# First attention: where the output projection waits for the four pieces of its weight

## The chip, the cores and the metric

One core of one Trainium2 chip runs the whole program in one launch. The metric is the device time in microseconds. The kernel before took 1580.31 us, the median of three runs (1579.23 to 1580.67).

## The reference

The reference computes four residual layers on x of shape (2, 512, 512): attention with 32 heads in 8 key/value groups, a gated feed-forward layer with ternary weights, a second attention with 32 small heads, and a routed low-rank layer. Only the first attention matters here. Cut to its core it is:

```python
q = (h @ wq.T)   # 32 heads of 128; h is the layer norm of x
k = (h @ wk.T)   # 8 heads of 128, each shared by 4 query heads
v = (h @ wv.T)
q, k = rotary(q), rotary(k)
scores = einsum(q, k) / sqrt(128) * scale + causal
attn = einsum(softmax(scores), v)          # (2, 512, 4096)
x = x + attn @ wo.T                        # wo: (512, 4096)
```

## The kernel before, in words

Every matrix product is done in three TensorE matmuls on values split into a high and a low part (`product`, line 59 on: lines 64, 65 and 66 are hi times hi, lo times hi, hi times lo). So every weight that arrives from HBM is split by GpSimd in two instructions, line 403 for the high part and line 405 for the low part, before TensorE may use it; the second one counts `piece_split` up by one.

The first attention (`attention0_phase`) runs over 8 groups g, one for each key/value head. A group has 8 steps s, one for each unit of attention (2 batches times 4 query heads). Group 0 is written out, groups 1 to 6 are a loop, group 7 is written out, and 4 more steps follow it, in which only output projections are left. Each engine has its own program, and all orders are written out by hand; the engines meet in semaphores.

In a step TensorE does two score tiles of the next unit, two transposes (line 562, seven matmuls), then the side work of the step, then two more score tiles, half of a query projection, two parts of the attention output, a transpose and so on. The side work (`SIDE`) is keys in steps 0 and 4, values in steps 1 and 5, and the output projection (`make_out`) in steps 2, 3, 6 and 7. Steps 6 and 7 project batch 0 of this group, steps 2 and 3 batch 1 of the group before it. One step has two halves, that is two token tiles; each half sums four products, one for each head j, and each product is three matmuls of 512 columns. So `make_out` issues 12 matmuls for a half. After each half VectorE adds the bank to x (line 736).

The group's piece of the output weight comes in four pieces, one for each head j: `PIECES` gives ("wo", 0) and ("wo", 1) to step 4 and ("wo", 2) and ("wo", 3) to step 5. SP fetches each into one of five raw slots, and GpSimd splits it in that step: it does the low part of the query of the step before (line 421), then the pieces, then the sum of the next rotation (line 411). `free_for` lets it overwrite the output weight once the last output projection of the group before is done (step 3).

`make_out` has its waits in the first half of steps 2 and 6 alone: for the attended heads (`attended_split`, counted by VectorE), and for `piece_split` at the count of the fourth piece, both ahead of the first product. Step 2 uses the same weight as step 6 before it. There are 8 executions of step 6 with an output projection and 8 of step 2.

Of the kernel before, what the change touches and what calls it, by code (L numbers as in the profile page):

```python
# [29 lines left out]
PER_KV = HEADS0 // KV0  # L30
# [24 lines left out]
def wait(engine, semaphore, value):  # L55

    if isinstance(value, int) and value <= 0:
        return
    engine.wait_ge(semaphore, value)


def product(nc, out, left, right, start, stop):

    nc.tensor.matmul(out, left[0], right[0], start=start, stop=False)  # L64
    nc.tensor.matmul(out, left[0], right[1], start=False, stop=False)  # L65
    return nc.tensor.matmul(out, left[1], right[0], start=False, stop=stop)  # L66
# [146 lines left out]
def attention0_phase(nc, m):  # L213
    dram = m.dram
    with ExitStack() as ctx:
# [3 lines left out]
        def pair(what, shape):  # L219
            return sb(f"{what}_hi", shape, F32R), sb(f"{what}_lo", shape, F32R)  # L220

        def sem(what):
            return ctx.enter_context(nc.semaphore(f"a0_{what}"))
# [6 lines left out]
        wo = pair("wo", [P, PER_KV, D])  # L230
# [24 lines left out]
        piece_hi, piece_split = sem("piece_hi"), sem("piece_split")  # L255
# [30 lines left out]
        def piece_count(g, what, which):  # L286

            names = [x[:2] for x in PIECES]
            return len(FIRST_PIECES) + len(PIECES) * g + names.index((what, which)) + 1
# [33 lines left out]
        def wait_output_bank(pe, g, s, what, half):  # L323

            at = OUTPUTS.index((s, what, half)) - 2
            gb = g
            while True:
                if at < 0:
                    at, gb = at + len(OUTPUTS), gb - 1
                sb_, before, hb = OUTPUTS[at]  # L330
                if isinstance(gb, int) and gb < 0:
                    return
                if present(gb, sb_, before):
                    break
                at -= 2
            if before == "out":
                wait(pe, out_added, out_count(gb, sb_, hb))
            else:
                wait(pe, attended_split, GROUP * gb + sb_ + 1)
# [137 lines left out]
        def _(pe):  # L477
# [20 lines left out]
            def weights_ready(what, which, g):  # L498

                if isinstance(g, int) and g == 0 and what != "wo":  # L500
                    return FIRST_PIECES.index((what, which)) + 1
                if what == "wo":
                    if isinstance(g, int) and g == KV0 - 1:
                        return len(FIRST_PIECES) + len(PIECES) * g + which + 1
                    return piece_count(g, what, which)
                return piece_count(g - 1, what, which)
# [72 lines left out]
            def make_out(g, s, half):  # L579

                b = 1 if s < 4 else 0
                t = 2 * (s % 2) + half
                bank = OUTPUTS.index((s, "out", half)) % 2
                gw = g - 1 if b else g
                wait_output_bank(pe, g, s, "out", half)
                if half == 0 and s in (2, 6):
                    wait(pe, attended_split, GROUP * gw + PER_KV * (b + 1))
                    wait(pe, piece_split, weights_ready("wo", PER_KV - 1, gw))
                for j in range(PER_KV):
                    at = slice(t * P, (t + 1) * P)  # L590
                    last = product(nc, ps_out[:, bank, :], (attended[0][:, b, j, at], attended[1][:, b, j, at]),
                                   (wo[0][:, j, :], wo[1][:, j, :]), j == 0, j == PER_KV - 1)
                last.then_inc(out_made, 1)

            def step(g, s):
# [7 lines left out]
                if present(g, s, SIDE[s]):  # L603
                    if SIDE[s] == "out":
                        make_out(g, s, 0)
                        make_out(g, s, 1)
                    elif SIDE[s] == "keys":
                        make_keys(g, s)
                    else:
                        make_values(g, s)  # L610
# [1484 lines left out]
```

## Time and profile before

| | |
|---|---|
| median of 3 runs | 1580.31 us |
| the profiled execution's own time | 1577.87 us |
| its span, first to last instruction | 1576.0 us |
| TensorE matmul busy | 1457.7 us, 92% of the span |
| VectorE, ScalarE, GpSimd busy | 1020.9, 857.8, 536.7 us |
| mean granted TensorE clock | 0.977 of full speed |

Times in the rows count from the start of the span. In a row of the timeline "[1.79 <-POOL a_wo_lo L405]" means that the engine had been idle for 1.79 us before the instruction, and that line 405 on GpSimd released it. PE is TensorE's matmuls and PEld its weight loads; the load of a matmul's weights runs beside the matmul before it.

### The profile page before, as it was taken

The numbers are of one execution on the slowest core, as the hardware profiler recorded it, in microseconds if no ns is written. First come the engines' busy times: TensorE is split into PE (matmuls) and PEld (weight loads), VectorE is DVE, ScalarE is ACT, GpSimd is POOL, SyncE is SP. The second block draws the span as 40 slices with busy tenths as digits, with TensorE's granted clock in tenths as the row PEclk, the third lists the DMA queues.
The fourth block names the chain that finished last, engine by engine and source line by source line (L and its number), as shares of the span: only waits on it lengthen the run. The fifth ranks groups of instructions, "written<-read, shape, count | busy, mean of one in ns | idle before, by whom it ended". The sixth has DMA issues, their size and how long they took to land. (4 is left out here: it accounts for less than half of the span.)

```text
span 1576.0 us, 25393 instructions
## 1 busy us (share of the span) xinstructions
PE 1457.7 (92%) x7696; PEld 1205.1 (76%) x7696; DVE 1020.9 (65%) x2547; ACT 857.8 (54%) x2183; POOL 536.7 (34%) x467
## 2 busy tenths in 40 slices
PE   6899999999999999999887999998789899986798
PEld 4788888888888888888766888886677777764586
DVE  7767667676676766667645333354788888897643
ACT  2766555665556655566523323311888888894210
POOL 5563555545555455553310000023332214010600
PEclk9999999999999999999988999999999999997999
DMA  4010010101101000000002111106433434322000
GB/s 163 14 48 15 27 35 20 40 13 27 33 20 40 13 29 31 27 7 7 15 7 88 61 60 60 54 0 107 94 74 87 73 81 85 73 34 96 21 21 27
DMA packets 37517, 71.98 MB, mean 46 GB/s; under 512 B 4992, under 2 KB 5376, under 8 KB 36864
## 3 DMA queue, kind: packets, MB, share of 16 engines
q1 hardware_dynamic: 29664, 55.35, 11.4%
q0 software_dynamic: 7776, 15.73, 6.3%
q8 instruction: 33, 0.54, 0.1%
q14 instruction: 44, 0.36, 0.1%
HBM read 60.58 MB, written 10.49 MB: 45 GB/s over the span
## 5 line engine op out<-in xcount | busy, mean ns | idle before, releaser
L804 ACT ACTIVATE a_probs<-a_probs,a_least 128x512 f32<-128x512 f32 (+3 forms) x256 | 143.0, 559 | 179.6 <-DVE a_least L684 170.9
L411 POOL TENSOR_TENSOR a_rotated<-a_by_cos,a_by_sin 128x512 f32<-128x512 f32 x80 | 103.5, 1293 | 244.3 <-DVE a_by_sin L707 242.2
L692 DVE TENSOR_TENSOR a_probsT_lo<-a_ps_turn,a_probsT_hi 128x512 fp32r<-128x512 f32 (+3 forms) x256 | 118.7, 484 | 72.1 <-ACT a_probsT_hi L812 70.6
L812 ACT CAST a_probsT_hi<-a_ps_turn 128x512 fp32r<-128x512 f32 (+3 forms) x256 | 101.4, 426 | 100.9 <-PE a_ps_turn L562 100.8
L1702 ACT ACTIVATE a_probs<-a_probs,a_least 128x128 f32<-128x128 f32 (+3 forms) x256 | 142.2, 560 | 2.4 <-issue 1.5
L1590 DVE CUSTOM_DVE_ANT_0 a_probs<-f_ps_gate,a_causal 128x128 f32<-128x128 f32 (+3 forms) x256 | 116.9, 486 | 31.2 <-PE f_ps_gate L1447 21.2
L864 ACT ACTIVATE a_probs<-a_probs,a_inverse 128x128 f32<-128x128 f32 (+3 forms) x256 | 123.2, 553 | 8.6 <-DVE a_inverse L717 7.5
L64 PE MATMUL a_ps_out<-a_wo_hi,a_attended_hi 128*128 128x512 f32 x256 | 105.4, 412 | 17.6 <-POOL a_wo_lo L405 15.4
L684 DVE CUSTOM_DVE_ANT_0 a_probs<-a_ps_score,a_causal 128x512 f32<-128x512 f32 (+2 forms) x192 | 101.0, 551 | 29.4 <-PE a_ps_score L66 29.3
L421 POOL TENSOR_TENSOR a_query_lo<-a_rotated,a_query_hi 128x512 fp32r<-128x512 f32 x64 | 82.6, 1290 | 107.9 <-ACT a_query_hi L824 107.9
L736 DVE TENSOR_TENSOR x<-a_ps_out,x 128x512 f32<-128x512 f32 x64 | 44.3, 691 | 104.3 <-PE a_ps_out L66 104.3
L64 PE MATMUL a_ps_proj<-xT_hi,a_wq_hi 128*128 128x512 f32 x256 | 109.1, 426 | 1.5 <-DVE a_values_lo L712 1.5
L1598 DVE TENSOR_TENSOR a_probsT_lo<-f_ps_out,a_probsT_hi 128x384 fp32r<-128x384 f32 (+1 forms) x192 | 108.9, 596 | 2.4 <-ACT a_probsT_hi L1711 2.2
L1460 PE MATMUL f_ps_out<-ident,a_probs 128*128 128x128 f32 x640 | 93.7, 278 | 14.0 <-ACT a_probs L1702 13.8
L562 PE MATMUL a_ps_turn<-ident,a_probs 128*128 128x128 f32 x640 | 102.3, 275 | 2.5 <-ACT a_probs L864 2.5
L65 PE MATMUL a_ps_out<-a_wo_lo,a_attended_hi 128*128 128x512 f32 x256 | 102.5, 400 | 0.0
L66 PE MATMUL a_ps_out<-a_wo_hi,a_attended_lo 128*128 128x512 f32 x256 | 102.4, 400 | 0.0
L1711 ACT CAST a_probsT_hi<-f_ps_out 128x384 fp32r<-128x384 f32 (+1 forms) x192 | 85.8, 511 | 30.4 <-PE f_ps_out L1460 30.3
L66 PE MATMUL a_ps_proj<-xT_hi,a_wq_lo 128*128 128x512 f32 x256 | 100.7, 393 | 0.0
L65 PE MATMUL a_ps_proj<-xT_lo,a_wq_hi 128*128 128x512 f32 x256 | 100.3, 392 | 0.0
L1460 PEld LDWEIGHTS f_ps_out<-ident,a_probs 128*128 128x128 f32 x640 | 74.3, 142 | 25.7 <-ACT a_probs L1702 11.4
L1447 PE MATMUL f_ps_gate<-a_stacked_k,a_stacked_q 128*128 128x128 f32 (+3 forms) x256 | 76.3, 377 | 16.5 <-DMA a_stacked_k<-in_slope 7.8
(276 smaller groups left out, 4129.2 us busy)
## 6 DMA issues: line engine op xcount, KB each, us to landing
a_raw<-in_wq SPq DMA_DIRECT2D x36, 256.0 KB, 2.7
a_raw<-in_wo SPq DMA_DIRECT2D x36, 256.0 KB, 2.6
a_stacked_q<-a_spill_q POOLq DMA_DIRECT2D x48, 128.0 KB, 5.1
a_stacked_k<-a_spill_k POOLq DMA_DIRECT2D x24, 256.0 KB, 5.1
f_raw<-in_gate SPq DMA_DIRECT2D x14, 256.0 KB, 2.7
f_raw<-in_up SPq DMA_DIRECT2D x14, 256.0 KB, 2.9
f_raw<-in_down SPq DMA_DIRECT2D x14, 256.0 KB, 3.6
a_raw<-in_wk SPq DMA_DIRECT2D x12, 256.0 KB, 2.9
```

The costliest lines, as they stand in the source:

```text
L64: nc.tensor.matmul(out, left[0], right[0], start=start, stop=False)
L65: nc.tensor.matmul(out, left[0], right[1], start=False, stop=False)
L66: return nc.tensor.matmul(out, left[1], right[0], start=False, stop=stop)
L411: nc.gpsimd.tensor_tensor(rotated[:], by_cos[:], by_sin[:], ALU.add).then_inc(rotation_added, 1)
L562: last = nc.tensor.transpose(ps_turn[:, t % 2, (i - t) * P:(i - t + 1) * P], probs[:, u % 2, at:at + P], m.ident[:])
L692: nc.vector.tensor_tensor(probsT[1][:, t % 2, 0:w], ps_turn[:, t % 2, 0:w], probsT[0][:, t % 2, 0:w].bitcast(F32), ALU.subtract).then_inc( ...
L804: nc.scalar.activation(tile, tile, ACT.Exp, bias=least[:, slot, i:i + 1], scale=-1.0, accum_out=total[:, slot, i:i + 1]).then_inc(exp_done, 1)
L864: nc.scalar.activation(tile, tile, ACT.Copy, scale=inverse[:, slot, i:i + 1]).then_inc(probs_ready, 1)
L1460: last = nc.tensor.transpose(ps_turn[:, t, to:to + P], probs[:, u % 4, at:at + P], m.ident[:])
L1590: nc.vector.tensor_tensor_reduce(out=probs[:, u % 4, at:at + w], in0=ps_score[:, i % 2, 0:w], in1=causal[:, SEQ - w:SEQ], scale=-float(HD1 ...
L1598: nc.vector.tensor_tensor(probsT[1][:, u % 2, at], ps_turn[:, t, 0:TURNED_WIDTH[t]], probsT[0][:, u % 2, at].bitcast(F32), ALU.subtract).t ...
L1702: nc.scalar.activation(tile, tile, ACT.Exp, bias=least[:, u % 4, i:i + 1], scale=-1.0, accum_out=total[:, u // 4 % 2, i, u % 4:u % 4 + 1]) ...
```

## The change

The wait for the fourth piece ahead of the first product is taken out. In its place each of the four products has a wait of its own, ahead of its three matmuls, for the count of its own piece. As before this is in the first half of steps 2 and 6 alone. The wait for the attended heads stays where it is, and no other engine's program is touched.

```diff
                 if half == 0 and s in (2, 6):
                     wait(pe, attended_split, GROUP * gw + PER_KV * (b + 1))
-                    wait(pe, piece_split, weights_ready("wo", PER_KV - 1, gw))
                 for j in range(PER_KV):
+                    if half == 0 and s in (2, 6):
+                        wait(pe, piece_split, weights_ready("wo", j, gw))
                     at = slice(t * P, (t + 1) * P)
                     last = product(nc, ps_out[:, bank, :], (attended[0][:, b, j, at], attended[1][:, b, j, at]),
                                    (wo[0][:, j, :], wo[1][:, j, :]), j == 0, j == PER_KV - 1)
```

## Rows read from the trace of the kernel before

**Rows 1.** The page: busy us (share of span) xinstructions, by engine.
```profile
PE 1457.7 (92%) x7696; PEld 1205.1 (76%) x7696; DVE 1020.9 (65%) x2547; ACT 857.8 (54%) x2183; POOL 536.7 (34%) x467
```

**Rows 2.** Who waited for whom on TensorE: us in total, times, longest us.
```profile
PE a_ps_out L64 <- POOL a_wo_lo L405: 15.4, 8, 3.3
```

**Rows 3.** Stretch by stretch: length, busy us by engine, clock; one group of the loop.
```profile
158.00:256.00 98.00, 96.31 (x522) 82.33 (x522) 66.15 (x162) 58.88 (x152) 51.23 (x41) 1.00 0.10 28
```

**Rows 4.** Weight loads in time: start us, us, then the instruction; group 1, step 6.
```profile
204.62 0.86 PEld L562 LDWEIGHTS a_ps_turn<-ident,a_probs 128*128 128x128 f32 x7
207.41 0.19 PEld L64 LDWEIGHTS a_ps_out<-a_wo_hi,a_attended_hi 128*128 128x128 f32 x1 [1.93 <-POOL a_wo_lo L405]
```

**Rows 5.** The same view of group 2, step 2.
```profile
254.57 0.86 PEld L562 LDWEIGHTS a_ps_turn<-ident,a_probs 128*128 128x128 f32 x7
255.40 0.19 PEld L64 LDWEIGHTS a_ps_out<-a_wo_hi,a_attended_hi 128*128 128x128 f32 x1
...
257.37 0.19 PEld L64 LDWEIGHTS a_ps_out<-a_wo_hi,a_attended_hi 128*128 128x128 f32 x1
```

**Rows 6.** GpSimd in time, group 1, steps 4 and 5.
```profile
190.94 1.29 POOL L411 TENSOR_TENSOR a_rotated<-a_by_cos,a_by_sin 128x512 f32<-128x512 f32 x1 [2.35 <-DVE a_by_sin L707]
...
196.17 1.29 POOL L405 TENSOR_TENSOR a_wo_lo<-a_raw,a_wo_hi 128x512 fp32r<-128x512 f32 x1
...
203.48 1.30 POOL L405 TENSOR_TENSOR a_wo_lo<-a_raw,a_wo_hi 128x512 fp32r<-128x512 f32 x1
...
206.09 1.27 POOL L405 TENSOR_TENSOR a_wo_lo<-a_raw,a_wo_hi 128x512 fp32r<-128x512 f32 x1
```

**Rows 7.** The weight loads of group 0, step 6.
```profile
106.63 0.86 PEld L562 LDWEIGHTS a_ps_turn<-ident,a_probs 128*128 128x128 f32 x7
109.49 0.19 PEld L64 LDWEIGHTS a_ps_out<-a_wo_hi,a_attended_hi 128*128 128x128 f32 x1 [2.00 <-issue]
```

**Rows 8.** Matmuls in time, group 1, step 6.
```profile
207.42 0.50 PE L64 MATMUL a_ps_out<-a_wo_hi,a_attended_hi 128*128 128x512 f32 x1 [1.69 <-POOL a_wo_lo L405]
...
208.22 0.39 PE L64 MATMUL a_ps_out<-a_wo_hi,a_attended_hi 128*128 128x512 f32 x1
...
208.92 0.40 PE L64 MATMUL a_ps_out<-a_wo_hi,a_attended_hi 128*128 128x512 f32 x1
...
214.52 0.40 PE L64 MATMUL a_ps_proj<-xT_hi,a_wq_hi 128*128 128x512 f32 x1
...
215.21 0.40 PE L64 MATMUL a_ps_out<-a_probsT_hi,a_values_hi 128*128 128x512 f32 x1
```

**Rows 9.** VectorE, ScalarE and GpSimd in time, behind that stall.
```profile
210.53 0.69 DVE L736 TENSOR_TENSOR x<-a_ps_out,x 128x512 f32<-128x512 f32 x1 [2.35 <-PE a_ps_out L66]
...
214.40 0.51 ACT L804 ACTIVATE a_probs<-a_probs,a_least 128x256 f32<-128x256 f32 x1 [5.12 <-DVE a_least L684]
...
220.62 1.29 POOL L411 TENSOR_TENSOR a_rotated<-a_by_cos,a_by_sin 128x512 f32<-128x512 f32 x1 [7.37 <-DVE a_by_sin L707]
```

**Rows 10.** GpSimd in time, group 7, step 5: the fourth piece.
```profile
794.43 1.26 POOL L405 TENSOR_TENSOR a_wo_lo<-a_raw,a_wo_hi 128x512 fp32r<-128x512 f32 x1
```

**Rows 11.** Weight loads of group 7, step 6.
```profile
790.71 1.55 PEld L562 LDWEIGHTS a_ps_turn<-ident,a_probs 128*128 128x128 f32 x7
795.80 0.29 PEld L64 LDWEIGHTS a_ps_out<-a_wo_hi,a_attended_hi 128*128 128x128 f32 x1 [3.55 <-issue]
...
799.19 0.19 PEld L64 LDWEIGHTS a_ps_out<-a_wo_hi,a_attended_hi 128*128 128x128 f32 x1
```

**Rows 12.** Stretches around it: PE, PEld, DVE, ACT, POOL, clock, DMA share, GB/s.
```profile
785.00:788.70 3.70, 0.74 (x6) 0.74 (x7) 0.69 (x3) 2.60 (x9) 2.97 (x3) 1.00 0.28 71
788.70:792.10 3.40, 3.40 (x14) 3.01 (x14) 1.65 (x4) 1.72 (x4) 1.47 (x2) 0.50 0.16 46
792.10:795.50 3.40, 0.39 (x3) 0.16 (x2) 1.28 (x4) 2.27 (x6) 2.34 (x2) 1.00 0.08 31
795.50:798.90 3.40, 3.07 (x7) 2.51 (x8) 0.00 (x0) 0.00 (x0) 0.19 (x1) 0.51 0.00 0
```

## The prediction, made before the change was built

> **What bounds the kernel now.** I read the page first. TensorE's matmuls fill 92% of the span, VectorE comes next at 65% and GpSimd at 34% [rows 1]. The reader should not take the 92% as a bound everywhere, but as a reason to ask where TensorE stops. The list of waits answers that for the place of the change: its longest entry in the whole program is the first matmul of the output projection, which waited for GpSimd's low part of the output weight, 15.4 us in 8 times [rows 2]. That is one stall in each of the eight executions of step 6, and none in step 2, where the weight has been there for half a group. Then the stretches: in the 98 us of one group TensorE is busy for 96.31 us, at the full clock (1.00, that is 2.4 GHz) [rows 3]. Idle time is 98 - 96.31 = 1.69 us, about the size of that group's stall (worked out below). So inside the loop TensorE's own work sets the pace, plus this single stall, and what shortens the stall shortens the group unless another wait takes its place.
>
> **How long the stall is, counted on the weight loads.** A matmul's end is modelled, so I count between starts of weight loads. In step 6 of group 1 the loads of the seven transposes begin at 204.62, and the first load of the output projection came at 207.41 [rows 4]. In step 2, with nothing to wait for, it comes 255.40 - 254.57 = 0.83 us after the first of the transposes [rows 5]. So it was due at 205.45, and the stall is 1.96 us.
>
> **When the pieces are there.** GpSimd ends the second piece at 196.17 + 1.29 = 197.46, the third at 203.48 + 1.30 = 204.78 and the fourth at 206.09 + 1.27 = 207.36 [rows 6]. TensorE resumed 0.05 us after the last of these. So at 205.45 three of four pieces are ready, and only the fourth is late.
>
> **When the fourth is needed.** Without a wait, the first load of head 3's product comes 257.37 - 255.40 = 1.97 us after that of head 0 [rows 5]. From 205.45 that is 207.42. The release, as seen before, is at 207.41. So the fourth wait is met at the very moment it is reached, and the whole 1.96 us goes. This is tight: if GpSimd were 0.3 us later against TensorE, 0.3 us of each stall would stay.
>
> **Is the release still at that moment?** GpSimd's chain up to the fourth piece starts with a rotation for which it had been idle 2.35 us, released by VectorE, which had waited for TensorE's keys of step 4 [rows 6]. The chain is thus hung on TensorE's own progress, not on GpSimd's throughput, and moves forward with it. The same holds in each of the groups 1 to 6, where nothing but this stall separates TensorE from running through.
>
> **Group 0.** Due at 106.63 + 0.83 = 107.46, came at 109.49 [rows 7]: a stall of 2.03 us. Head 3 is due 1.97 later, at 109.43, and the release is at 109.49, so 0.06 remains and 1.97 us goes.
>
> **What the added waits cost.** 16 first halves (8 of step 6, 8 of step 2) with four waits in place of one: 48 more. Each sits on the first weight load of a product, with the loads and matmuls of the next products, and after them the score tiles, queued behind it; VectorE's addition to x and ScalarE's exponentials wait for those. Lower bound: the attention output product also has a wait for VectorE on its load and follows a projection of 512 columns; its matmul starts 215.21 - 214.52 = 0.69 us after the first of the three matmuls before it, and three such matmuls in flow take 208.92 - 208.22 = 0.70. So a met wait costs 0. Below 0 it cannot go, since a wait gives TensorE no work less. Upper bound: the product right behind the real stall took 208.22 - 207.42 = 0.80 us against those 0.70, so 0.10 more [rows 8], and 48 x 0.10 = 4.8 us. I take 0, the row nearest in form, a met wait behind matmuls of 512 columns.
>
> The Trainium skill bears on this, in "TensorE: Matmul & The Clock Gate", section "Step-by-step: what each phase is for": TensorE's queue pulls a weight load ahead of the matmuls in flight. Read against this change, a load that carries a wait might not be pulled ahead; the row above shows none of that for a met wait, and by the rule taken strictly each wait would show its load of 0.19 us. The rival of 9.1 us below is worked out from rows without it.
>
> **What is late next.** Behind the stall come two halves of output projection, 24 matmuls that need no other engine. VectorE had been idle 2.35 us before the first addition, ScalarE 5.12 us before its next exponential, GpSimd 7.37 us before its next rotation [rows 9]. All three have more slack than the 1.96 us that goes, and VectorE's does not gate TensorE at all there. Step 2 runs through the same side work without a stall, which is the sign that the other engines keep up.
>
> **Group 7.** Here GpSimd ends the fourth piece at 794.43 + 1.26 = 795.69 [rows 10], behind a transfer, and the stall is longer. The transposes begin at 790.71 and their seven loads last 1.55 [rows 11], so TensorE is free at about 792.2. It can then do heads 0 to 2 in 1.97 us, to about 794.2, and waits 1.6 us for the fourth. Head 3's first load then comes at 795.80, where head 0's came before. In the kernel before it came at 799.19 [rows 11]. The gain is 3.39 us. It is more than three products of 0.70, because these ran at half clock before.
>
> The rows on the clock: after a stretch with 0.74 us of matmuls in 3.70 the clock was 0.50 (1.2 GHz), after a full stretch it was 1.00, and after the stretch with 0.39 us of matmuls in 3.40 it was 0.51 again [rows 12]. In the changed kernel that third stretch holds some 2 us of products, and the stalls of 1.7 us inside the loop never cost the clock (1.00 in [rows 3]). So I take the full clock behind the remaining wait. Should it still be half, then heads 3 and after run at half pace for up to 3.4 us, 1.7 us is lost, and the gain is 1.7.
>
> The Trainium skill says the same of the place ("TensorE: Matmul & The Clock Gate", "Loop structure matters more than you think"): products done between two waits keep the clock up where one long wait lets it fall to half. By that rule the sum would be the one taken here, and by its opposite 1.7 us less; the trace of before shows only the long wait and its half clock.
>
> **The sum.** Groups 1 to 6: 6 x 1.96 = 11.8. Group 0: 1.97. Group 7: 3.39. Added waits: 0. Together 17.1 us. Everything behind the first attention hangs on its end and moves forward by as much. The profiled execution took 1577.87 us, 1.87 more than its span of 1576.0, so it would take 1560.7. It lies 2.4 us under the median of the runs shown; the saving is the same in each, so I forecast 1580.3 - 17.1 = 1563.2 us.
>
> **Rivals.**
> 1. *The loads lose their lead.* Each added wait exposes its weight load, 0.19 us [rows 4]: 48 x 0.19 = 9.1 us given back, gain 8.0, time 1572.3. With 0.10 each it is 4.8, and 1568.0. For it: the 0.80 us product behind the stall. Against it: the met wait at 215.21 that cost nothing [rows 8].
> 2. *The stall comes back elsewhere.* If another engine's chain sets the period of a group, the 2 us reappear as a wait of TensorE for scores or probabilities in step 6 or 7, and only group 7's 3.4 us or less is kept: 1577 to 1580. That also stands for a change that does not do what it says, where some earlier count is not reached in time and head 0 waits almost as long. Against: the idle times in [rows 9] and the times in [rows 6].
> 3. *The added waits drain the engine: slower.* If a wait on a load is only passed once all matmuls in flight are done, each costs the end of the last matmul (0.40 - 0.23 = 0.17, the pitch being 0.70 / 3), the bare weight load (0.19), the 0.05 from release to load and the 0.10 of the slow first product: 0.51 us. Its place is the three inner borders of each of the 16 first halves. 48 x 0.51 = 24.5 us, less the 17.1: 1587.7. The change turns slower than before from 17.1 / 48 = 0.36 us a wait on. Against: again the row at 215.21.
>
> **How the numbers follow.** Forecast 0.82, with a range of its own from 1560.8 to 1565.5: half clock in group 7 (+1.7) and a few tenths of each stall left upward, and downward 2 us for half-clock stretches that fall elsewhere or not at all. Rival 1: 0.09. Rival 2: 0.07. Rival 3: 0.02. The range reaches into rival 1 at its cheaper end, 1560.5 to 1567.5, which leaves out under 2 in 10. A measurement of this kernel can tell from no change about 0.2%, 3.2 us. Faster by more than that: forecast, rival 1 and a little of rival 2, 0.92. Within: most of rival 2, 0.06. Slower: 0.02.
>
> **What would show it.** In the list of waits the 15.4 us of the output projection on GpSimd fall to under 2 us, all in group 7 and some hundredths in the others. A group's period shortens by 1.96 us. In step 6 head 0's first load follows the transposes by 0.83 us, and head 3's follows head 0's by 1.97 to 2.0. In step 2 the pitch of products stays 0.70; 0.8 or 0.9 there speaks for rival 1, 1.2 for rival 3. In group 7 the clock behind the fourth wait reads 1.00. A new entry of 2 us a group among TensorE's waits, or a product in step 6 that waits for piece 3 by more than 0.3 us, would make the prediction wrong.

## The result

The changed kernel took 1562.05 us, the median of five runs (1560.6 to 1563.06), against 1580.31 before (1576.68 to 1582.09). The ratio is 0.9889, with a 95% interval of 0.9875 to 0.9903. That is 18.3 us less, where 17.1 was forecast. The profiled execution took 1563.06 us against 1577.87, which is 14.8 less. One later execution of the kernel before was slow (1669.9 us, at a granted clock of 0.837) and counts in no comparison here.

The page of the changed kernel, its span and its busy times:

```profile
span 1561.2 us, 25411 instructions
PE 1457.9 (93%) x7696; PEld 1205.7 (77%) x7696; DVE 1021.4 (65%) x2547; ACT 857.5 (55%) x2183; POOL 536.8 (34%) x467
```

TensorE's busy time is what it was [rows 1]; only idle time went. The entry that stood first among TensorE's waits [rows 2] is gone. Of GpSimd's output weight the list of waits keeps one entry, of the weight loads, 0.6 us in all, which is the wait in group 7 shown further down:

```profile
PEld a_ps_out L64 <- POOL a_wo_lo L405: 0.6, 1, 0.6
```

Weight loads of group 1, step 6, which answer to [rows 4], with the first load of head 0 and of head 3:

```profile
203.74 0.86 PEld L562 LDWEIGHTS a_ps_turn<-ident,a_probs 128*128 128x128 f32 x7
204.57 0.19 PEld L64 LDWEIGHTS a_ps_out<-a_wo_hi,a_attended_hi 128*128 128x128 f32 x1
...
206.58 0.19 PEld L64 LDWEIGHTS a_ps_out<-a_wo_hi,a_attended_hi 128*128 128x128 f32 x1
```

Head 0 follows the transposes by 0.83 us, as in the step without a stall [rows 5]. Head 3 follows head 0 by 2.01 us, against 1.97 in flow. GpSimd's last instruction for the fourth piece, which answers to [rows 6]:

```profile
205.23 1.30 POOL L405 TENSOR_TENSOR a_wo_lo<-a_raw,a_wo_hi 128x512 fp32r<-128x512 f32 x1
```

It ends at 206.53, and head 3's load starts 0.05 later. So the fourth piece still comes last and just in time, 0.04 us late by the loads. In step 2, where every wait is met, the first loads of the four products stand at 252.50, 253.08, 253.77 and 254.48 us, 1.98 us from the first to the last against 1.97 in [rows 5]. So the added waits do not stretch the products. The period of a group, read from the transposes of step 6 in groups 2 and 3, fell to 395.77 - 299.83 = 95.94 us:

```profile
299.83 0.93 PE L562 MATMUL a_ps_turn<-ident,a_probs 128*128 128x128 f32 x7
395.77 0.93 PE L562 MATMUL a_ps_turn<-ident,a_probs 128*128 128x128 f32 x7
```

In the kernel before, the same two rows stand at 302.72 and 400.64, 97.92 apart. The idle times that answer to [rows 9] are:

```profile
207.68 0.69 DVE L737 TENSOR_TENSOR x<-a_ps_out,x 128x512 f32<-128x512 f32 x1 [0.37 <-PE a_ps_out L66]
...
211.55 0.51 ACT L805 ACTIVATE a_probs<-a_probs,a_least 128x256 f32<-128x256 f32 x1 [3.11 <-DVE a_least L685]
...
217.77 1.30 POOL L411 TENSOR_TENSOR a_rotated<-a_by_cos,a_by_sin 128x512 f32<-128x512 f32 x1 [5.34 <-DVE a_by_sin L708]
```

Each engine's slack shrank by just the 2 us (2.35 to 0.37, 5.12 to 3.11, 7.37 to 5.34), and none reached zero. That is why no new wait appeared.

Group 7, step 6, the load of head 3, which answers to [rows 11]:

```profile
783.17 0.19 PEld L64 LDWEIGHTS a_ps_out<-a_wo_hi,a_attended_hi 128*128 128x128 f32 x1 [0.56 <-POOL a_wo_lo L405]
```

The clock in stretches around it (columns as in [rows 12]):

```profile
774.20:781.00 6.80, 5.60 (x20) 5.13 (x21) 2.81 (x9) 4.01 (x12) 3.94 (x4) 0.50 0.13 39
781.00:784.40 3.40, 3.29 (x14) 2.39 (x13) 1.19 (x3) 1.61 (x5) 2.04 (x2) 0.99 0.00 0
784.40:787.80 3.40, 3.40 (x19) 2.85 (x18) 1.28 (x3) 0.00 (x0) 0.00 (x0) 1.00 0.00 0
```

The fourth wait did not take the clock down, as forecast. But the 2.4 GHz came later than before: the half clock behind the wait of step 5 lasted through the transposes and into head 0, so TensorE came to the fourth wait later and waited 0.56 us and not 1.6.

**Where the profile's 14.8 us are.** I cut the span at two landmarks: the first load of group 0's step 6 transposes (107.78 now, 106.63 before, [rows 7]) and the first transpose of the layer norm behind the attention (819.71 now, 837.41 before).

| stretch | before | after | difference |
|---|---|---|---|
| start to group 0, step 6 | 106.63 | 107.78 | +1.15 |
| to the end of the first attention | 730.78 | 711.93 | -18.85 |
| the rest of the program | 738.6 | 741.5 | +2.9 |

The middle stretch alone holds the changed place, and it gained more than the sum. In the first and the third no instruction differs; there half-clock stretches fell otherwise. Ahead of group 0's step 6 the changed kernel had 6.8 us of half clock, from 43.8 us on, and the kernel before 3.4. In the second attention, for instance, the changed kernel had one long one, where the kernel before had two shorter ones with full clock between:

```profile
1078.00:1091.70 13.70, 9.66 (x39) 8.31 (x38) 9.88 (x31) 9.90 (x24) 0.00 (x0) 0.50 0.00 0
```

```profile
1095.90:1102.70 6.80, 5.65 (x24) 4.78 (x23) 6.00 (x14) 3.10 (x6) 0.00 (x0) 0.50 0.00 0
1102.70:1106.20 3.50, 0.84 (x2) 0.37 (x2) 2.26 (x9) 3.49 (x10) 0.00 (x0) 0.99 0.00 0
1106.20:1109.60 3.40, 3.34 (x14) 3.24 (x15) 1.30 (x6) 2.37 (x8) 0.00 (x0) 0.51 0.00 0
```

### The profile page after: what moved, and what is told of

The parts are those of the page before. It is cut to its first block and busy times, and to the rows that moved or that the text cites. A ratio compares the mean times of both kernels' runs of the same rounds, so it can differ in the third digit from the quotient of the medians.

```text
span 1561.2 us, 25411 instructions
## 1 busy us (share of the span) xinstructions
PE 1457.9 (93%) x7696; PEld 1205.7 (77%) x7696; DVE 1021.4 (65%) x2547; ACT 857.5 (55%) x2183; POOL 536.8 (34%) x467
## 5 line engine op out<-in xcount | busy, mean ns | idle before, releaser
L562 PEld LDWEIGHTS a_ps_turn<-ident,a_probs 128*128 128x128 f32 x640 | 80.6, 142 | 14.0 <-ACT a_probs L865 3.0
```

Of the source, the lines that this page charges most:

```text
L562: last = nc.tensor.transpose(ps_turn[:, t % 2, (i - t) * P:(i - t + 1) * P], probs[:, u % 2, at:at + P], m.ident[:])
```

## The experiments

Nine kernels ran. The first four shared one set of runs of the kernel before (1580.15), the next two another (1580.8), the last three a third (1581.59).

**Two waits in place of four.**

```diff
-                    if half == 0 and s in (2, 6):
-                        wait(pe, piece_split, weights_ready("wo", j, gw))
+                    if half == 0 and s in (2, 6) and j in (0, PER_KV - 1):
+                        wait(pe, piece_split, weights_ready("wo", PER_KV - 2 if j == 0 else j, gw))
```

> In place of four waits a first half has two: for the third piece ahead of head 0, for the fourth ahead of head 3. Theory (only the fourth piece is late, and met waits are free): as fast as the changed kernel, 1562 us within 0.2%, and the same 1.97 us from head 0's to head 3's first load in step 6. Rival (a met wait costs 0.10 to 0.19 us of lost weight-load lead): 32 waits fewer than the changed kernel, 3.2 to 6.1 us faster than it, 1556 to 1559.

Measured: 1561.53 us (1561.25 to 1566.09), ratio 0.9886 (0.9869 to 0.9903), the same as the changed kernel. Only the fourth piece's wait earns anything in step 6. In group 7 it also shows the wait as forecast, because here the clock came back just as the transposes began, at 776.1:

```profile
780.36 0.50 PE L64 MATMUL a_ps_out<-a_wo_hi,a_attended_hi 128*128 128x512 f32 x1 [1.11 <-POOL a_wo_lo L405]
```

Its loads had been idle 1.55 us, and behind it the clock read 1.00 from 780.4 to 789.7 us.

**Waits everywhere.**

```diff
-                    if half == 0 and s in (2, 6):
-                        wait(pe, piece_split, weights_ready("wo", j, gw))
+                    wait(pe, piece_split, weights_ready("wo", j, gw))
```

> Every half of every output projection has the four waits, not only the first halves of steps 2 and 6: 64 halves by 4, so 192 more waits than in the changed kernel, all of them met. Theory (met waits are free): 1562 us within 0.2%, and 0.70 us from one product to the next in every half. Rival (0.10 to 0.19 us each): 19 to 36 us more, 1581 to 1598. A draining engine (0.51 each) would give 98 us more, 1660.

Measured: 1561.56 us (1560.95 to 1563.78), ratio 0.9883 (0.9866 to 0.9901). 192 waits more cost nothing that can be told. The runs spread by about 3 us, which over 192 waits leaves at most some 0.015 us for one. The loop says it more sharply. From the transposes of step 6 in group 1 to those in group 6 it took 680.71 - 201.02 = 479.69 us:

```profile
201.02 0.86 PEld L562 LDWEIGHTS a_ps_turn<-ident,a_probs 128*128 128x128 f32 x7
680.71 0.86 PEld L562 LDWEIGHTS a_ps_turn<-ident,a_probs 128*128 128x128 f32 x7
```

In the changed kernel the same five periods took 683.45 - 203.74 = 479.71 us, with 120 waits less. The first and the third rival fall, and the doubt that a waiting load loses its lead with them.

**All of the wait ahead of head 1.**

```diff
-                    if half == 0 and s in (2, 6):
-                        wait(pe, piece_split, weights_ready("wo", j, gw))
+                    if half == 0 and s in (2, 6) and j in (0, 1):
+                        wait(pe, piece_split, weights_ready("wo", 0 if j == 0 else PER_KV - 1, gw))
```

> Head 0 waits for the first piece, head 1 already for the fourth, heads 2 and 3 for nothing. Theory (a stall shrinks by just what is issued ahead of the wait): from head 0's first load to head 1's is 0.58 us in flow, so 0.58 of the 1.96 us goes in groups 0 to 6, 4.1 us, and in group 7 the first load of head 1 comes at the release in place of head 0's, 1.0 us. Together 5.1: 1575 us, and stalls of 1.38 us left in the loop ahead of head 1. Rival (the split of the wait as such releases the engine, by a better position of its queue): most of the 18 us, under 1567.

Measured: 1571.84 us (1570.5 to 1577.21), ratio 0.9943 (0.993 to 0.9956). It is between the two theories' numbers and 3 us past mine. The trace, matmuls at head 1 in groups 2 and 3:

```profile
305.66 0.51 PE L64 MATMUL a_ps_out<-a_wo_hi,a_attended_hi 128*128 128x512 f32 x1 [1.04 <-POOL a_wo_lo L405]
402.91 0.50 PE L64 MATMUL a_ps_out<-a_wo_hi,a_attended_hi 128*128 128x512 f32 x1 [1.07 <-POOL a_wo_lo L405]
```

The period is 97.25 us (97.22 in every other group) against 97.92 to 97.94 before, so some 0.70 per group is gained, not 0.58: a whole product. The middle stretch (from 108.36 to 833.21, 724.85 us) is 5.9 us shorter than before, which is 7 x 0.70 + 1.0. The rest of the 8.3 us by the medians lies outside what I can read: the profiled execution, at 1577.21, was the longest of the six. The mechanism stands, with 0.58 as a wrong size.

**Group 7 alone.**

```diff
-                    if half == 0 and s in (2, 6):
-                        wait(pe, piece_split, weights_ready("wo", j, gw))
+                    if half == 0 and s in (2, 6) and (j == 0 or isinstance(g, int) and g == KV0 - 1 and s == 6):
+                        each = isinstance(g, int) and g == KV0 - 1 and s == 6
+                        wait(pe, piece_split, weights_ready("wo", j if each else PER_KV - 1, gw))
```

> The four waits in group 7's step 6 alone; groups 0 to 6 and all of step 2 wait for the fourth piece as before. Theory: group 7 is worth 3.4 us by the release, and up to 1.7 more or less by which stretches run at half clock: 1576.9 us, within 1575 to 1579; the stalls of 1.7 us stay in groups 0 to 6. Rival (group 7's stall is only passed on to the waits of steps 6 and 7 behind it): no gain, 1580.

Measured: 1578.5 us over twelve runs (1571.77 to 1583.05), ratio 0.9981 (0.9969 to 0.9993). It is within the range expected, but the gain is 1.65 us where 3.3 was the middle. The stalls of 1.7 us stayed in groups 0 to 6. What the release gave can be read alone: from the transposes of step 6 in group 6 to the first load of head 3 in group 7 it took 796.60 - 695.40 = 101.20 us, against 799.19 - 694.29 = 104.90 before, which is 3.7 less. But two half-clock stretches stand behind the remaining wait of 2.45 us, the first of them 1.1 us behind the release, and TensorE is busy throughout both:

```profile
797.70:801.10 3.40, 3.40 (x10) 2.63 (x9) 0.60 (x1) 0.00 (x0) 0.00 (x0) 0.50 0.00 0
818.20:821.60 3.40, 3.40 (x10) 2.62 (x9) 2.61 (x8) 0.00 (x0) 0.00 (x0) 0.50 0.02 5
```

So the time from head 3's release to the landmark can be set against the number of such stretches in it, the same work each time: 783.17 to 819.71 = 36.5 us with none (changed kernel); 780.36 to 818.50 = 38.1 with one (two waits); 799.19 to 837.41 = 38.2 with one (before); 796.61 to 836.24 = 39.6 with two (this one). One such stretch is worth 1.6 us. Group 7 is worth the 3.7 us of the release and then 1.6 us up or down by the clock. The profiled execution, 1583.05 us, was the longest of the twelve.

**GpSimd later.** The changed kernel with one instruction more.

```diff
+        spare = sb("spare", [P, 512])
 ...
                 pool.wait_ge(raw_in[slot], 16 * landed)
+                if (what, which) == ("wo", PER_KV - 1):
+                    nc.gpsimd.tensor_tensor(spare[:], zeros[:], zeros[:], ALU.add)
```

> The changed kernel with one instruction more on GpSimd (a sum of zeros into a spare tile, 128 by 512, 1.29 us at a pitch of 1.25) ahead of the split of the fourth piece in each group. Theory (the fourth piece comes just when head 3 needs it, with no slack): each group gets a stall of about 1.25 us ahead of head 3, 8 times, 10.0 us: 1572 us. Rival (slack is hidden behind the products, 0.5 us or more): 4 us or less lost, under 1566. Rival (GpSimd's lateness piles up from group to group): over 1575.

Measured: 1570.6 us (1567.6 to 1574.84), ratio 0.9934 (0.9916 to 0.9953), 8.5 above the changed kernel. The instruction itself was shorter than I took it to be, 1.04 us, a pitch of 1.00:

```profile
202.36 1.04 POOL L404 TENSOR_TENSOR a_spare<-a_zeros 128x512 f32<-128x512 f32 x1
```

Each group takes 396.11 - 299.26 = 96.85 us, 0.91 more. So the lateness does not pile up, and nearly all of it shows: the fourth piece has no slack.

**The fetches of group 7 at once.** The changed kernel with:

```diff
                     if last:
-                        wait(sp, piece_split, len(FIRST_PIECES) + len(PIECES) * g + done)
+                        wait(sp, piece_split, len(FIRST_PIECES) + len(PIECES) * g)
```

> The changed kernel, but SP fetches the four pieces of group 7's output weight at once, without waiting for each split before the next fetch. Theory: GpSimd's two waits for these transfers (3.3 and 2.8 us) go. The first ends TensorE's wait for the transposed probabilities in step 5 (3.5 us, which hangs on ScalarE's query_hi behind GpSimd) all but some tenths, the second the last 0.56 us ahead of head 3. With the half clock of 3.4 us behind that wait gone too, 1.7 us, together 5 to 6 us: 1556.5 us. Rival (the query rotation of step 4, not the transfer, holds the chain): under 1.5 us, 1561.

Measured: 1557.68 us (1557.59 to 1558.31), ratio 0.9852 (0.9833 to 0.9871). This is the fastest version, 4.4 us under the changed kernel. GpSimd's two idle times for transfers are gone. The wait of step 5 went by half only, and the wait ahead of head 3 altogether:

```profile
772.90 0.38 PE L64 MATMUL a_ps_out<-a_probsT_hi,a_values_hi 128*128 128x256 f32 x1 [1.76 <-DVE a_probsT_lo L693]
```

I had forecast some tenths of it left; 1.76 us stay. GpSimd's rotation is not what holds them. In the changed kernel ScalarE had waited 2.83 us for it before its high part of the query; here it does that part without a wait and waits for VectorE's last score tile instead (first row the changed kernel, then two rows of this one):

```profile
773.13 0.62 ACT L825 CAST a_query_hi<-a_rotated 128x512 fp32r<-128x512 f32 x1 [2.83 <-POOL a_rotated L411]
```

```profile
769.48 0.60 ACT L825 CAST a_query_hi<-a_rotated 128x512 fp32r<-128x512 f32 x1
771.64 0.40 ACT L805 ACTIVATE a_probs<-a_probs,a_least 128x128 f32<-128x128 f32 x1 [0.99 <-DVE a_least L685]
```

Behind that exponential ScalarE copies the transposed probabilities, which VectorE and then TensorE need. VectorE itself had been busy from 766 to 771.6 us with no gap above 0.2 us. So the next limit of this step is VectorE's work, not a transfer.

**All of the wait ahead of head 2.** After the first six I corrected the size: a load held up by x should cost less than x, since in flow it leads its matmul by 0.23 us.

```diff
-                    if half == 0 and s in (2, 6):
-                        wait(pe, piece_split, weights_ready("wo", j, gw))
+                    if half == 0 and s in (2, 6) and j in (0, 2):
+                        wait(pe, piece_split, weights_ready("wo", 1 if j == 0 else PER_KV - 1, gw))
```

> Head 0 waits for the second piece, head 2 for the fourth. Corrected theory (a weight load runs 0.23 us ahead of its matmul in flow, so a load held up by x costs x - 0.13, and every product issued ahead of the wait saves its whole 0.70 us): a group of the loop takes 97.94 - 1.40 = 96.54 us. First theory (only the distance between loads counts): head 2's load comes 1.27 us after head 0's in flow, so 97.94 - 1.27 = 96.67 us.

Measured, one execution: 1574.25 us, and a period of 397.11 - 300.55 = 96.56 us:

```profile
300.55 0.93 PE L562 MATMUL a_ps_turn<-ident,a_probs 128*128 128x128 f32 x7
397.11 0.92 PE L562 MATMUL a_ps_turn<-ident,a_probs 128*128 128x128 f32 x7
```

That is the corrected number (96.54) and not the first (96.67). The total tells little here: from the landmark behind the attention, 825.33, to the end of the span at 1572.4 it took 747.1 us, 5.6 more than the changed kernel for the same instructions.

**GpSimd a little later.** As above, with 64 columns.

```diff
-                    nc.gpsimd.tensor_tensor(spare[:], zeros[:], zeros[:], ALU.add)
+                    nc.gpsimd.tensor_tensor(spare[:, 0:64], zeros[:, 0:64], zeros[:, 0:64], ALU.add)
```

> The changed kernel with a short instruction more on GpSimd ahead of the split of the fourth piece (64 columns in place of 512). Say it holds GpSimd up by d, read from the distance of the splits around it. Corrected theory: a group of the loop grows by d - 0.13 less what head 3's wait had over (0.04 us late already), so by about d - 0.1; with d at 0.15 to 0.3 us that is 96.0 to 96.2 us in place of 95.95. First theory: it grows by the whole d.

Measured, one execution: 1565.2 us. The splits around the new instruction are 0.25 us further apart. The loads of group 1, step 6 (transposes, head 0, head 3):

```profile
203.50 0.86 PEld L565 LDWEIGHTS a_ps_turn<-ident,a_probs 128*128 128x128 f32 x7
204.33 0.19 PEld L64 LDWEIGHTS a_ps_out<-a_wo_hi,a_attended_hi 128*128 128x128 f32 x1
...
206.61 0.19 PEld L64 LDWEIGHTS a_ps_out<-a_wo_hi,a_attended_hi 128*128 128x128 f32 x1 [0.35 <-POOL a_wo_lo L408]
```

Head 3's load is 206.61 - 204.33 - 1.97 = 0.31 us late. The period is 395.94 - 299.81 = 96.13 us, 0.19 more than 95.94. With a delay of 0.25 the corrected theory wants 0.15 and the first one 0.25, so this one profile lies nearer the corrected theory but does not hit it. By the loads, 0.12 us of lateness was free.

**The fetches alone, in the kernel before.** The same edit of the fetches, with the old wait ahead of head 0.

> The kernel before with the fetch of group 7's four output weight pieces at once, and the old wait for the fourth piece ahead of head 0. Theory: the wait for transposed probabilities in step 5 shrinks from 3.3 to 1.8 us and the stall ahead of head 0 from 3.3 to about 1.1 us, together 3.7, and one or two half-clock stretches of 1.7 us may go: 1580.2 less 3.7 to 7: 1573 to 1576.5 us. Groups 0 to 6 keep 97.94 us each. Rival (the transfers only matter together with the wait for each piece): 1580 us.

Measured: 1571.66 us (1569.76 to 1573.66), ratio 0.9937 (0.992 to 0.9953), which is 1.3 us faster than the range that I gave. The wait of step 5 is 1.76 us, the stall ahead of head 0 in group 7 0.89 us:

```profile
786.08 0.38 PE L64 MATMUL a_ps_out<-a_probsT_hi,a_values_hi 128*128 128x256 f32 x1 [1.76 <-DVE a_probsT_lo L692]
790.00 0.47 PE L64 MATMUL a_ps_out<-a_wo_hi,a_attended_hi 128*128 128x512 f32 x1 [0.89 <-POOL a_wo_lo L405]
```

The middle stretch (106.20 to 830.17) is 6.8 us shorter, at the upper end of what I gave it. By the medians it is 9.9, 3 more than I can account for. The two edits overlap: alone they bring 18.3 and 9.9 us, together 23.1 (1580.8 less 1557.68).

## Why the prediction was right

- **The bound.** TensorE plus one stall per group. The slack of the other three engines shrank by 2.0 us each and stayed above zero.
- **The stall and what it gives.** 1.96 us a group forecast, 97.92 - 95.94 = 1.98 measured. Splitting the wait is not what helps by itself; where the last wait stands decides. Ahead of head 1 it gave 0.70, ahead of head 2 97.92 - 96.56 = 1.36, ahead of head 3 all of it. Each product that is issued ahead of the wait takes its own length off the stall.
- **Just in time.** Head 3's load came 0.04 us late. That GpSimd has no slack was shown by making it later: 0.91 us a group for an instruction of 1.00. The prediction said that 0.3 us of lateness would leave 0.3 of the stall; 0.31 left 0.19. That step was mis-sized, and it worked in favour of the change. It rested on distances between loads alone and left out the 0.23 us by which a load leads its matmul.
- **Added waits at 0.** Shown with 192 more: five periods of the loop took 479.69 us with 120 more waits in them and 479.71 without. The 0.10 us of the product behind a stall is not a cost of the wait as such.
- **Group 7, the release.** 3.4 us were forecast for the release. From the transposes of group 6's step 6 to head 3's load in group 7 the changed kernel took 783.17 - 683.45 = 99.72 us against 104.90, 5.2 less. With 1.98 of it for group 6's own stall, 3.2 is left for group 7.
- **Group 7, the clock.** The wait left was 0.56 us and not 1.6, so the changed kernel did not test the forecast that the full clock outlasts a wait of 1.6. The kernel with two waits did (1.55 us by the loads, and 1.00 behind it). It is no rule: with group 7 alone the loads waited 2.88 us, and half clock began 1.1 us behind the release, where with GpSimd later they waited 2.52 us and the clock read 1.00 for the next 3.4 us. The kernel before had a half-clock stretch in heads 0 to 2, which the forecast counts [rows 11, 12], and one more at 819 to 823 us, which the changed one lacked in its profile; that is 1.7 us beyond the sum, and chance: the kernels with two waits and with waits everywhere, which have the same wait ahead of head 3, each had one such stretch again (38.1 us from head 3 to the landmark in both, against 36.5).
- **The total.** 13.7 + 3.4 = 17.1 against 18.3 by the medians and 18.9 in the middle stretch of the profiles. The 18.9 are 12.0 in groups 0 to 5, 5.2 from group 6 to head 3 in group 7, and 1.7 behind it, and the last of these no term forecast. Without it 17.2 stand against the 17.1 of the sum, in this one profile. The 1.2 us left over by the medians is within the spread of the runs, 5.4 us before and 2.5 after.

What stays open is why the medians of the head 1 kernel and of the fetches alone lie 2.4 and 3 us under what their profiled executions explain. The rest of the program, the same instructions in all, took from 738.6 to 747.1 us in the eleven profiles, so a single profile can't settle it.

## What to carry to other kernels

Where an engine waits for the last of several pieces ahead of work that uses them one by one, compare two times: how late the last piece is, and how long the work on the earlier ones lasts. If the second is the longer, a wait for each piece removes the whole stall. Met waits between matmuls of 512 columns cost nothing here. Check the slack of every engine behind the stall before counting on it, and measure such an edit by the period of the loop or a landmark close to it, since the total carries the luck of the clock.

## What the runs showed of the hardware

- A weight load held up in the middle of a run of 512-column matmuls costs 0.12 to 0.16 us less than its lateness: 0.31 late cost 0.19, 1.06 (206.07 against 205.01) cost 0.91, 1.45 (head 1, 208.44 against 206.99) cost 97.25 - 95.94 = 1.31. An account that fits: the load's lead over its matmul, 0.23 us, is used up first, and 0.10 comes back in the slower first product. Behind the transposes, where the load leads its matmul by only 0.03 us (255.40 and 255.43), nothing was free: the stall of 1.96 us cost 1.98.
- Met semaphore waits ahead of products of 512 columns cost nothing: 120 more of them in five periods of the loop left 479.69 us against 479.71.
- The part of the program behind the first attention varied by 8.5 us between executions of the same instructions, half of the whole effect measured here. The granted clock did not fall to half in the same stretches each time.
- On GpSimd a sum of 128 x 512 with one tile as both inputs and an fp32 output took 1.04 us, against 1.29 for the splits; with 64 columns 0.29 us.
